# Top-2 expert layer: rows sorted by expert through DRAM in place of all experts on all rows

## The reference

```python
h = _ln(x, ln_g, ln_b)
logits = h @ rw.T + rb
vals, idx = jax.lax.top_k(logits, K)          # K = 2 of E = 8 experts
gates = jax.nn.softmax(vals, axis=-1)
h1 = gelu(einsum('nd,efd->enf', hf, fc1_w) + fc1_b)      # DFF = 512
eo = einsum('enf,edf->end', h1, fc2_w) + fc2_b
gathered = eo[idx_f, arange(N)[:, None], :]
return x + (gathered * gates_f[..., None]).sum(axis=1)
```

## Time and profile before

| | |
|---|---|
| median of 3 runs | 301.21 us (301.18 to 311.05) |
| the profiled execution | 302.3 us |
| its span, first to last instruction | 300.6 us |
| mean granted TensorE clock | 0.949 of full speed |
| TensorE busy | 277.4 us (92%) |
| VectorE, ScalarE, POOL busy | 170.4, 169.0, 56.9 us |
| chain that ended last, by engine | PE 73%, DVE 15%, issue 6%, ACT 4% |

### The profile page before, as it was taken

How to read it: one execution, slowest core, us unless ns; L and a number is a source line. 1 busy time by engine, 2 the same in 40 slices (tenths; PEclk the granted TensorE clock), 3 DMA queues, 4 the chain that set the end, 5 groups by cost and what they waited for, 6 DMA issues and landing times.

```text
span 300.6 us, 4742 instructions
## 1 busy us (share of the span) xinstructions
PE 277.4 (92%) x1691; PEld 167.9 (56%) x1694; DVE 170.4 (57%) x333; ACT 169.0 (56%) x225; POOL 56.9 (19%) x99
## 2 busy tenths in 40 slices
PE   7879899998999899997696999999999999999994
PEld 2344323423334232334133647969799989898984
DVE  3899889879999774577426776222122821211112
ACT  1424645847778678947280289478644644425350
POOL 2650018328022405023400212000001000000000
PEclk9999779869999899999799599999999999999999
DMA  7003137720000012000021000000000010000001
GB/s 236 18 24 82 25 84 266 304 59 3 2 2 4 2 37 74 0 7 5 3 70 35 4 4 0 2 2 0 2 1 2 1 35 2 0 2 0 2 0 35
DMA packets 7015, 10.81 MB, mean 36 GB/s; under 512 B 1429, under 2 KB 4945, under 8 KB 6737
## 3 DMA queue, kind: packets, MB, share of 16 engines
q1 hardware_dynamic: 6705, 10.08, 10.8%
q10 hardware_dynamic: 288, 0.43, 0.5%
HBM read 6.10 MB, written 0.52 MB: 22 GB/s over the span
## 4 chain that ended last, share of the span: by engine, by line
PE 73%; DVE 15%; issue 6%; ACT 4%; POOL 1%; DVEq 0%; POOLq 0%; ACTq 0%
PE ps_r L954 19%; PE ps_o L886 7%; DVE row_max L656 7%; PE ps_r L866 5%; PE ps_r L939 5%; PE ps_r L941 5%; PE ps_r L940 5%; PE ps_r L826 4%; DVE row_max L660 3%; PE ps_x L749 3%; PE ps_o L893 3%; PE ps_o L898 3%; PE ps_r L837 2%; ACT probs L529 2%; DVE x_hat L596 2%
## 5 line engine op out<-in xcount | busy, mean ns | idle before, releaser
L529 ACT ACTIVATE probs<-ps_r 128x1024 f32<-128x1024 f32 (+1 forms) x88 | 83.9, 985 | 33.8 <-PE ps_r L866 26.7
L656 DVE TENSOR_REDUCE row_max<-ps_r 128x2 f32<-128x1024 f32 x64 | 75.1, 1220 | 7.8 <-PE ps_r L826 6.7
L557 ACT ACTIVATE hidden<-ps_r,cols_sb 128x512 f32<-128x512 f32 x64 | 42.0, 688 | 38.3 <-PE ps_r L941 37.7
L954 PEld LDWEIGHTS ps_r<-fc_sb,hidden 128*128 128x128 f32 x512 | 59.4, 192 | 2.5 <-issue 1.3
L954 PE MATMUL ps_r<-fc_sb,hidden 128*128 128x128 f32 x512 | 60.4, 275 | 0.0
L725 DVE SCALAR_TENSOR_TENSOR x_sb<-ps_r,gate,x_sb 128x128 f32<-128x128 f32 x64 | 18.0, 344 | 59.8 <-PE ps_r L954 59.8
L886 PE MATMUL ps_o<-probs,v_aug 128*9 128x512 f32 x256 | 36.3, 647 | 0.0
L826 PE MATMUL ps_r<-k_tile,q_tile 32*128 32x512 f32 x128 | 32.5, 515 | 2.2 <-DVE row_max L656 1.3
L866 PE MATMUL ps_r<-q_tile,k_tile 32*128 32x512 f32 x128 | 30.3, 506 | 3.8 <-DVE row_max L656 3.1
L660 DVE TENSOR_REDUCE row_max<-ps_r 128x4 f32<-128x616 f32 x32 | 23.9, 796 | 10.8 <-PE ps_r L837 10.3
L826 PEld LDWEIGHTS ps_r<-k_tile,q_tile 32*128 32x128 f32 x128 | 13.3, 197 | 24.2 <-issue 14.1
(11 more groups left out here) (136 smaller groups left out, 344.0 us busy)
## 6 DMA issues: line engine op xcount, KB each, us to landing
q_tile<-q_part SPq DMA_DIRECT2D x36, 64.0 KB, 2.1
hidden<-fc_w SPq DMA_DIRECT2D x1, 2048.0 KB, 7.7
fc_sb<-fc_w SPq DMA_DIRECT2D x1, 2048.0 KB, 13.7
k_tile<-k_part SPq DMA_DIRECT2D x12, 64.0 KB, 2.1
x_sb<-x SPq DMA_DIRECT2D x2, 256.0 KB, 4.7
fc_sb<-w_rep SPq DMA_DIRECT2D x1, 512.0 KB, 5.3
q_tile<-max_rows SPq DMA_DIRECT2D x32, 8.0 KB
out<-x_sb SPq DMA_DIRECT2D x2, 256.0 KB, 2.3
```

The costliest lines, as they stand in the source:

```text
L529: nc.scalar.activation(probs[:, i:i + w], ps_r[:, slot("s", r), 0:w], ACT.Exp, scale=SCALE).then_inc(s_read, 1)
L557: ins = nc.scalar.activation(hidden[:, FC * (x_e % 2) + c], ps_r[:, slot("s", r), a], ACT.Gelu, bias=col(C_FC1_B + FC * (x_e % E) + c))
L656: nc.vector.tensor_reduce(heads[:, 2 * pair:2 * pair + 2, t], ps_r[:, slot("m", r)], AX.X, ALU.max).then_inc(m_read, 1)
L954: mm = nc.tensor.matmul(ps_r[:, slot("m", r), 0, t * D:t * D + D], hidden[:, FC * (n % 2) + c, t * P:t * P + P], fc2_sb[:, e, c], start=(c ...
```

## The change

The expert layer no longer computes every expert for every row. The steps in its place, for each batch n:

- **"place"**: TensorE multiplies the marks of the chosen experts (chosen, 0 or 1) with an upper triangle of ones and with ones: the sums say how many rows before this one chose the expert. From them VectorE works out, for the two picks of each row, its place among 1024 places sorted by expert (at), and for each of 15 cells (eight tiles of 128 places plus seven borders between experts) its tile and its expert, as whole numbers (weight_at, expert_at, tile_at, bias_at).
- **"scat"**: POOL issues eight transfers with an address per row (four tiles by two picks); each writes 128 rows of 130 numbers into the DRAM buffer sorted_rows.
- **"loadx"**: SP reads the 1024 sorted rows back, 532 KB, as xs.
- **"xT"**: eight transposes on TensorE, two evacuations by ScalarE with the layer's scale and bias; VectorE works out from the rows' tags where each result row has to go (to).
- **"regs"**: TensorE (two reads), ScalarE and SP (one each) read the cells' numbers into registers. They wait for cells_ready.
- **"stage"**: SP loads 256 KB of first-layer weights of a cell's expert into one of three buffers.
- **"e1"** and **"e2"**: for a cell, four products of 128 x 128, four Gelus of 128 x 128, four products of 128 x 128, and a VectorE copy to one of eight output buffers. The tile, the bias and the second layer's weights are addressed by registers.
- **"est"**: POOL sends a cell's 128 result rows, with an address per row, to the DRAM buffer expert_rows.
- **"egat"**: when all 15 of a batch are sent, SP reads 1024 rows back in two halves and VectorE adds them to x_out, each times its gate (eight operations); the store follows in two halves.

The weight splits, rows_split, the split products and the additions after each expert are gone. Filler steps go from 22 to 6. The second layer's weights come in eight pieces of 256 KB. The normalized rows go to a new buffer of two batches, x_rows. POOL fills some constants at the start ("clear:3"). The list of steps is written anew, the attention steps in it too; a line of it before and after:

```diff
-    fc1:9 fc2a:3 pv:45 fc2b:3 pv:44 oc:14 fc2a:4 fc2b:4 fc1:10-11 oT:14 fc1:12 osT:3 fc1:13 proj:3 ln:5 fc2a:5 hat:5
+    pv:44 oc:14 oT:14 loadx:0 osT:3 proj:3 ln:5 regs:0 stage:0-2 xT:0-1 e1:0-2 hat:5 hT:5 stage:3 e2:0-1 e1:3
+    router:1 stage:4-5 e2:2 gates:1 e1:4 stage:6 e1:5 stage:7 e2:3-4 stage:8 place:1 est:0 e1:6 est:1-2 e1:7 est:3
 @block.sync
+                elif kind == "loadx":
+                    sp.wait_ge(scattered[n], 16 * PICKS * QT)
+                    sp.dma_start(xs[:, n], sorted_rows[n].rearrange("(t p) c -> p t c", p=P)).then_inc(xs_loaded[n], 16)
+                elif kind == "regs":
+                    sp.wait_ge(cells_ready, n + 1)
+                    expert_of[n] = load_values(mybir.EngineType.SP, expert_at[0:1, n], E - 1)
+                elif kind == "stage":
+                    if n >= STAGES:
+                        sp.wait_ge(s_filled, S_RING["e1", n - STAGES] + 1)
+                    sp.dma_start(fc1_stage[:, n % STAGES], fc1_w.rearrange("d e f -> d (e f)")[:, bass.ds(expert_of[n // CELLS][n % CELLS] * FF, FF)])                         .then_inc(staged[n % STAGES], 16)
+                elif kind == "egat":
+                    for k in range(OUT_BUFS):
+                        sp.wait_ge(e_sent[k], 16 * len(range(k, CELLS * (n + 1), OUT_BUFS)))
...
+                    for h in range(2):
+                        sp.dma_start(y_sb[:, 4 * h:4 * h + 4], rows_of[:, 4 * h:4 * h + 4]).then_inc(y_loaded[n][h], 16)
 @block.gpsimd
-                elif kind == "fc1_split":
...
+                elif kind == "scat":
+                    pool.wait_ge(placed, n + 1)
+                    for t in range(QT):
+                        for k in range(PICKS):
+                            nc.gpsimd.indirect_dma_start(
+                                sorted_rows[n], bass.IndirectOffsetOnAxis(ap=at[:, n, k, t:t + 1], axis=0),
+                                x_rows[:, n, t], None).then_inc(scattered[n], 16)
+                elif kind == "est":
+                    b, i = n // CELLS, n % CELLS
...
+                    pool.wait_ge(e_ready, n + 1)
+                    nc.gpsimd.indirect_dma_start(
+                        expert_rows[b], bass.IndirectOffsetOnAxis(ap=to[:, b, i:i + 1], axis=0),
+                        e_out[:, n % OUT_BUFS], None).then_inc(e_sent[n % OUT_BUFS], 16)
 @block.scalar
+                elif kind == "e1":
+                    r, i = S_RING[step], n % CELLS
+                    if n >= HIDDEN:
+                        act.wait_ge(m_filled, M_RING["e2", n - HIDDEN] + 1)
+                    for c in range(FC):
...
+                        ins = nc.scalar.activation(
+                            hidden[:, n % HIDDEN, c * P:c * P + P], ps_r[:, slot("s", r), c // 2, c % 2 * P:c % 2 * P + P],
+                            ACT.Gelu, bias=cols_sb[:, bass.ds(bias_of[n // CELLS][i] + (C_FC1_B + c), 1)])
                     ins.then_inc(s_read, 1)
 @block.vector
-                elif kind == "rows_split":
...
+                elif kind == "xT":
+                    b, half = n // 2, n % 2
+                    if half == 0:
+                        dve.wait_ge(xs_loaded[b], 16)
...
+                elif kind == "e2":
+                    r = M_RING[step]
...
+                    if n >= OUT_BUFS:
+                        dve.wait_ge(e_sent[n % OUT_BUFS], 16 * (n // OUT_BUFS))
                     dve.wait_ge(m_filled, r + 1)
...
+                    nc.vector.tensor_copy(e_out[:, n % OUT_BUFS], ps_r[:, slot("m", r), 0, 0:D]).then_inc(m_read, 1)
 @block.tensor
-                        nc.tensor.matmul(ps_r[:, to, a], fc1_high[:, e, chunk], rows_part[b][:, 0], start=True, stop=False)
...
+                elif kind == "e1":
+                    b, i, r = n // CELLS, n % CELLS, S_RING[step]
+                    pe.wait_ge(staged[n % STAGES], 16 * (n // STAGES + 1))
...
+                    to_slot = wait_for_slot("s", r)
+                    for c in range(FC):
+                        mm = nc.tensor.matmul(ps_r[:, to_slot, c // 2, c % 2 * P:c % 2 * P + P],
+                                              fc1_stage[:, n % STAGES, c * P:c * P + P], place_of,
+                                              start=True, stop=True)
...
+                elif kind == "e2":
...
+                    pe.wait_ge(s_read, S_RING["e1", n] + 1)
+                    to_slot = wait_for_slot("m", r)
+                    for c in range(FC):
+                        mm = nc.tensor.matmul(ps_r[:, to_slot, 0, 0:D], hidden[:, n % HIDDEN, c * P:c * P + P],
+                                              fc2_at[:, bass.ds(weights_of[b][i] + c * P, P)],
+                                              start=c == 0, stop=c == FC - 1)
```

373 lines of the change are left out of this document (260 added, 113 removed).

## The result

The changed kernel takes 288.15 us (median of 5, 286.95 to 295.66) against 302.15 before (five runs, three of them those of the table of the kernel before): the ratio of the two is 0.957, with an interval of 0.951 to 0.964. It is faster by 4.3%; the forecast was 271 us, 10% less. The sign was right and the time lies in the range, but nearer to the rival of half clock (292) than to the forecast. The profiled execution took 290.2 us for a span of 288.3. Most kernels here have executions 1.5% or more above their own fastest, which the medians take in and the column "the rest" of the table of experiments, a mean, leaves out. Apart from these, times still spread by a few us (here from 286.95 us at a mean granted clock of 0.894 to 290.19 at 0.871), so profiles are compared by distances inside one execution, with the times beside them.

What follows compares the result with a forecast made beforehand. TensorE's dense expert layer bounds the last 124 us; 106 us of products give way to 28, leaving a chain through eight transfers. Its steps sum to a span of 270.6, run 272.3, median 271 us; range 252 to 296.

Steps and rivals of the forecast that it cites:

- the rival of half clock: TensorE at half clock through the cells, 2.5 us a cell: plus 21.4, 292 us; chance 0.14.
- The pace of a cell: Expert cells: 1.7 us each, with TensorE's eight products at 0.94 us at full clock; bounds 1.13 and 2.5.
- 32 x 0.117: Dense expert layer before the change: an expert's 128-column products on TensorE, part of its 6.6 us.
- step 4: Batch 0's transposes and evacuations, in all 2.1 us, to 201.7; first products 0.6, table 1.28: first Gelu at 203.6.
- step 5: Batch 1's normalization, transposes (0.6 us), router, ranks, gates and places, queued behind batch 0's work: placed at 215.9.
- step 6: Batch 1's scatters 9.6 + 2.3 us, read back 3.8, transposes 2.1, first products 0.6: to 234.3.
- The new wait at the register reads: Batch 1's cell numbers, read amid batch 0's cells, stop engines until about 217.5: 2 us later, covered by 2.6 us.
- The read back: Batch 1's sorted rows, read by SP right after the scatters land: 3.8 us.
- The price of a scatter: POOL's indirect transfers: 1.2 us each, entering the sum 17 times; landing takes 2.3 us.
- POOL never became the bound: Rival: POOL's 46 queued transfers bind, 307 us at 2.2 us each; chance 0.08 at 1.8 to 2.2, 0.14 above.
- POOL's splits: Weight splits slowing two normalizations on VectorE: removal gains 3.0 us up to batch 0's ranks, bounds 0 and 4.3.

Runs made afterwards that it cites:

- half the products: Changed kernel with each cell doing two of the four products of each layer: median 282.10 us, by the rest 279.99.
- constants: Changed kernel with constant addresses on TensorE for batch 1 instead of register reads of cell numbers: median 285.87 us, by the rest 283.64.
- the router's experiment: Changed kernel with batch 1's normalization, transposes, router and placing moved ahead of and between batch 0's first cells: median 291.90 us.
- the read back early: Changed kernel with only batch 1's read back moved ahead of the loads for cells 13 and 14 in SP's queue: median 287.58 us.
- filler: Changed kernel with ten and sixteen extra products of 512 columns into free PSUM where TensorE waits: median 288.57 us.
- combined: Changed kernel with one register read a batch, extra products, later gathering and store, earlier placing products of batch 0: median 286.40 us, ratio 0.9445 to the kernel before.
- reads: Changed kernel with batch 1's register reads of cell numbers moved behind the read back of its rows: median 287.98 us.
- the last experiment: Four more register reads of a constant list on SP: fifteen numbers took 1.92 us ahead of POOL's scatters, 1.56 beside them; five 0.75, ten 1.18.

## Why the prediction was wrong, step by step

- **The pace of a cell** is the step that failed: "TensorE: eight products 0.94 us at full clock". The 0.117 us of the earlier trace rows is the spacing of rows, and a float32 product is two rows. A cell is 16 rows, 1.79 us at full clock. The 1.7 that I took came near it only because I had put in half clock and exposed register waits. What hung on it was the wrong part: that TensorE has work for half of each cell. It has none to spare, and the "32 x 0.117" of an expert was right only as a count of rows. What the mistake was worth, half the products shows: with about the work that I had priced, the kernel takes 280 to 282 us, 6 to 8 of the 17 us between 288 and 271. The other 9 to 11 lie in steps 4 to 6.
- **Batch 0's first cell (step 4)**: 5.0 us lost from the first scatter to the first Gelu. I took transposes and first products at full clock and right behind the rows; they waited 2.6 us for ps_x and for batch 0's register reads, and ran at half clock.
- **Batch 1 queued behind batch 0 (step 5)**: 6.4 us late, 3.4 of them from step 4. I gave its transposes 0.6 us right after its normalization; on TensorE they stand behind three cells' first products, 5.48 us at half clock, and its router and placing products behind more cells.
- **The new wait at the register reads (step 6)** was seen, but priced as the wait for the numbers (2 us, covered). The reads themselves, which I had at nothing, cost TensorE two of 3.7 to 3.8 us; 5.62 show, and some 1.5 more at half clock behind them (2.07 and 2.47 us for eight and sixteen rows, against 1.06 and 1.95). Constants in their place gave 2.3 us of the median back, 4.6 by the rest.
- **The read back (step 6)** was taken at its landing. It stands in SP's queue behind the weights of cells 13 and 14: 4.5 us late, and in the router's experiment more than 11. Alone this wait was worth little: with the read back early TensorE itself was behind. I named what is queued behind the register reads, but not what the read back is queued behind.
- **The price of a scatter** was right: 1.26 us from start to start against 1.2, landing 2.3 as taken; so POOL never became the bound. The Trainium skill's figure for a POOL transfer, about 1 us ("DMA: Bandwidth & Descriptors", section "Latency and other measured facts"), is for the first byte and not for how long a transfer holds POOL; put in its place, as the prediction tried, 1.0 would have been too little, since the trace has 0.96 of work and 0.30 between. In the same way SP's issues of 0.45 to 0.68 us, which the prediction set beside the page's 0.6, are the time on SP; no row here shows a first byte.
- **POOL's splits** were worth more than the 3.0 us taken: 4.3 us of median when put back, and 8 to 9 when taken out of the kernel before. The way was right only in part: the two normalizations fell from 2.52 and 4.02 us to 2.11 and 2.09, not to 1.1, which is 2.3 us; where the rest is lost is not shown.
- **The half clock**: the rival gave 292 with this mechanism in all cells. That the time lies near it is luck: the trace has 0.50 from 165 to 177 and from 198 to 210, and 1.00 in batch 1's cells from 248 on. The rule of the Trainium skill cited for it ("TensorE: Matmul & The Clock Gate", section "Why this matters for your kernels"), of idle gaps before a drop, agrees with the drop within the 5.62 us of the reads. It does not account for the drop at about 162.7: from 157 on TensorE had waited at most 0.54 us at a time, and the wait of 1.42 us for VectorE's maxima, 162.5 to 163.9, had just begun. In the filler and combined runs the clock fell all the same, at about 170 and 171, with no wait above 0.53 us in the 12 us before. What decides is open.

No single queue held the kernel. By the medians, each experiment that freed one (reads, read back, clock, router) gave back 2.3 us at most of the 4 to 7 it freed; the runs do not exclude 4.6 for the constants. The traces show why: TensorE's cells, SP's in-order issues and the chain of scatters lie close together around batch 1's rows. TensorE waits 1.43 us for them in the changed kernel, 3.00 with constants, and not at all when the read back is early; and the clock falls again behind a wait that takes another's place. What stays open: why batch 1's reads take 3.3 to 4.1 us on three engines in every run where batch 0's take 1.6 to 1.8. Scatters alone are not the reason, and they take long with TensorE and ScalarE idle too. One rival was not tested: in each buffer of the code batch 1's fifteen numbers lie behind batch 0's, 60 bytes from its start, while all quick reads, those of the last experiment too, begin at the start of a buffer. Why the splits cost twice as much in the old list is open as well, and so is what the new order of the attention steps gave.

## What to carry to other kernels

Before pricing a product by its rows in a trace, divide the rows of its line by the products that the code issues there; a float32 product was two, a transpose one. In a queue that issues in order, a transfer on the critical chain is as late as the slowest wait ahead of it: look up what stands ahead of it on every engine that it crosses, not only what stands behind the new wait. And when one covered stall is removed, compare the slack of the next ones first: here three queues lay within a few us, and freeing any one of them was worth little. Count a wait of TensorE with what follows it: behind the 5.62 us here the next products took twice as long.

## What the runs showed of the hardware that was not expected

- A register read of fifteen numbers took 1.55 to 1.92 us on SP, 1.6 to 1.8 on TensorE and ScalarE, and 3.3 to 4.1 on all three in batch 1; five numbers took 0.75. The Trainium skill, "DMA: Bandwidth & Descriptors", section "Latency and other measured facts", gives such a load a floor of about 600 ns; the 0.75 agrees, as no run here goes lower.
- An indirect transfer of 128 rows costs POOL 0.96 us with 0.30 to the next, alike for 520-byte and 512-byte rows.
- Cells whose operands are addressed by registers run at the same 1.79 us as those with constant addresses.
- Behind 5.62 us without work TensorE's granted clock was 0.50 until about 234, and eight rows took 2.07 us instead of 1.06; behind a wait of 1.43 us at 242.9 it stayed at 1.00.
- Eight pairs of POOL passes over 128 x 512, some 15 us of POOL's work (8 x 1.88), cost 4.3 us of the kernel's time, 1.9 of them in one normalization beside them.
